# First score maximum ahead of the normalisation, and last score block ahead of the transposes with the maximum, in a fused cross-attention and mixture-of-experts kernel

## What is computed

```python
x = x + tanh(g_xattn) * xattn(layernorm(x), ctx, pos, pos, Wq, Wkv, Wout, bout)
x = x + tanh(g_ffn) * ffn(layernorm(x), sw1, sb1, sw2, sb2, rw1, rb1, rw2, rb2, router_w, router_b)
# xattn: q, k rotated; logits = q k^T / sqrt(8); w = softmax(logits); (w v) @ Wout + bout
# ffn: mean of 2 shared experts + sum over the 6 best of 32 routed experts of gate * expert(x)
```

## Time and profile before

| | |
|---|---|
| median of 3 runs | 428.22 us (428.2 to 428.32) |
| the profiled execution | 428.19 us, of which 426.2 us are the span from first to last instruction |
| busy: PE, DVE, ACT, POOL | 407.9, 264.4, 192.3, 154.5 us |
| granted PE clock over the span | 0.998 of full speed |
| DMA | 39.42 MB, mean 92 GB/s |

### The profile page before, as it was taken

The page is one execution under the profiler, slowest core; times in us unless marked ns, Lnnn a source line. Parts: engine busy times, 40 slices in busy tenths (PEclk is TensorE's granted clock), DMA queues, the critical chain, the costliest instruction groups (busy, mean ns, idle before and its releaser), DMA issues.

```text
span 426.2 us, 8239 instructions
## 1 busy us (share of the span) xinstructions
PE 407.9 (96%) x2651; PEld 315.9 (74%) x2651; DVE 264.4 (62%) x525; ACT 192.3 (45%) x371; POOL 154.5 (36%) x296
## 2 busy tenths in 40 slices
PE   7799999999999889999999999999999999999995
PEld 5477766666666567788888888888888888888884
DVE  7987888788887476365555555555555555555554
ACT  4784999889888736322222222222222222222221
POOL 8446333311001026344433443333433444444430
PEclk9999999999999999999999999999999999999999
DMA  8300000000000069399876333333333232333102
GB/s 227 87 2 0 2 3 2 2 2 2 2 2 2 2 179 339 95 240 262 242 221 210 98 98 98 96 99 90 94 93 105 77 105 86 95 97 96 49 0 99
DMA packets 27992, 39.42 MB, mean 92 GB/s; under 512 B 3665, under 2 KB 22145, under 8 KB 27969
## 3 DMA queue, kind: packets, MB, share of 16 engines
q1 hardware_dynamic: 26929, 39.11, 32.4%
q10 hardware_dynamic: 1040, 0.01, 0.1%
HBM read 37.93 MB, written 1.18 MB: 92 GB/s over the span
## 4 chain that ended last, share of the span: by engine, by line
PE 63%; DVE 1%; ACT 0%; DVEq 0%; issue 0%; ACTq 0%
PE psum L1255 30%; PE psum L1272 30%; PE psum L1231 1%; PE psum L968 0%; DVE attn L955 0%; PE psum L1225 0%; PE psum L1169 0%; PE psum L1292 0%; DVE xT L947 0%; DVEq L78 0%; PE psum L1157 0%; ACT Vx L583 0%; PE psum L1286 0%; PE psum L1125 0%; ACT lgT L646 0%
## 5 line engine op out<-in xcount | busy, mean ns | idle before, releaser
L669 ACT ACTIVATE hh<-hu 128x512 fp32r<-128x512 f32 x88 | 55.7, 633 | 182.1 <-DVE hu L936 182.1
L936 DVE SCALAR_TENSOR_TENSOR hu<-psum,b1cols,G 128x512 f32<-128x512 f32 x88 | 65.9, 750 | 105.2 <-PE psum L1255 101.7
L824 DVE TENSOR_REDUCE nmax<-psum 128x2 f32<-128x512 f32 x128 | 79.4, 683 | 11.1 <-PE psum L1067 10.4
L550 ACT ACTIVATE probs<-psum 128x512 f32<-128x512 f32 x128 | 69.4, 597 | 12.5 <-PE psum L1085 11.3
L1272 PE MATMUL psum<-hh,w2h 128*128 128x512 f32 x188 | 73.3, 390 | 0.0
L1272 PE MATMUL psum<-hh,w2l 128*128 128x512 f32 x188 | 73.2, 389 | 0.0
L1272 PE MATMUL psum<-hl,w2h 128*128 128x512 f32 x188 | 73.2, 389 | 0.0
L942 DVE SCALAR_TENSOR_TENSOR hl<-hu,hh 128x512 fp32r<-128x512 f32 x88 | 61.1, 696 | 9.2 <-ACT hh L669 9.2
L469 POOL CAST w2h<-w 128x256 fp32r x44 | 17.5, 398 | 126.7 <-PE psum L1272 126.7
L1255 PE MATMUL psum<-xTh,w1h 128*128 128x512 f32 (+1 forms) x188 | 58.1, 390 | 0.0
L1255 PE MATMUL psum<-xTh,w1l 128*128 128x512 f32 (+1 forms) x188 | 57.9, 389 | 0.0
(11 more groups left out here) (147 smaller groups left out, 487.0 us busy)
## 6 DMA issues: line engine op xcount, KB each, us to landing
w<-in_L_ffn_rw_dram SPq DMA_DIRECT2D x8, 1408.0 KB, 10.1
G<-gates_by_expert SPq DMA_DIRECT2D x40, 256.0 KB, 4.0
G<-gates_by_expert SPq DMA_DIRECT2D x8, 448.0 KB, 3.6
G<-gates_by_expert SPq DMA_DIRECT2D x8, 384.0 KB, 3.5
G<-gates_by_expert SPq DMA_DIRECT2D x8, 320.0 KB, 3.6
G<-gates_by_expert SPq DMA_DIRECT2D x8, 192.0 KB, 3.9
x_sb<-in_x_dram SPq DMA_DIRECT2D x4, 256.0 KB, 4.2
G<-gates_by_expert SPq DMA_DIRECT2D x8, 128.0 KB, 3.8
```

The costliest lines, as they stand in the source:

```text
L550: act.activation(probs[g % 2][:, :, n, :], st_bank(g, n)[:, :].rearrange("p (t q) -> p t q", t=TB), ACT.Exp, scale=SCALE).then_inc(exp_ok, 1)
L669: act.activation(hh[(SHT + j) % 2][:, cols], hu[2 * j + half][:, :], ACT.Relu).then_inc(rhh_ok, 1)
L824: dve.tensor_reduce(nmax[i % 2][:, :, n], S_BANK[(4 * i + n) % SB][:, :].rearrange("p (t k) -> p t k", t=TB), AX.X, ALU.max, negate=True). ...
L936: dve.scalar_tensor_tensor(out=hu[2 * (j % 2) + half][:, :], in0=H_BANK[2 * (j % 2) + half], scalar=b1cols[:, bass.ds(it * len(G) + j, 1)] ...
```

## The change

In DVE's loop the first maximum of a step comes ahead of `normalise` and of `residual`. In PE's loop, in odd steps from 7 on, `transposed_with_max` comes behind the last score block instead of ahead of it. Nothing is added or left out.

```diff
             for i in range(GROUPS + 4):
+                if i < GROUPS:
+                    row_max(i, 0)
                 if i >= 7 and i % 2:
                     normalise((i - 7) // 2)
                 if i - 1 in PROJ_STEPS:
                     residual(*PROJ_STEPS[i - 1])
                 if i < GROUPS:
-                    row_max(i, 0)
                     row_max(i, 1)
                     row_max(i, 2)
                     row_max(i, 3)
@@
                 if i >= 6 and i % 2 == 0:
                     outputs((i - 6) // 2)
-                if i >= 1:
+                outputs_read = i >= 7 and i % 2 == 1
+                if i >= 1 and not outputs_read:
                     transposed_with_max(i - 1)
                 if shifted:
                     pairs(score(i, 3), shifted_score(i - 2, 0))
                     pairs(shifted_score(i - 2, 1))
                 else:
                     pairs(score(i, 3))
+                if outputs_read:
+                    transposed_with_max(i - 1)
                 if weighted:
                     values(i - 3)
```

## The result

The changed kernel takes 436.81 us in the median (433.55 to 439.99, 4 executions), before it was 428.22: slower by the factor 1.0198, 95% interval 1.0154 to 1.0243. The forecast was 433.7 us with a range to 435.0. The direction was right, the time lies above the range. The four executions fall into two pairs: 433.55 and 433.91 us at a granted clock of 0.998 and 0.997, 439.70 and 439.99 us at 0.978. The first pair is the forecast. The profile is of an execution of the second pair (439.70 us), so it shows both what the forecast had and what it lacked. Executions more than 1.5% above their kernel's fastest are in the medians of this document, but not in its factors, which concerns one execution of `e9_residual_only_again` and two of `e7_longer_stall`.

What follows compares the result with a forecast made beforehand. The prediction took PE to bound the kernel, through the length of its attention steps. Odd steps +1.6 us and four residual stalls +3.9 us gave +5.5 us on 428.22, so 433.7 us, range 431.8 to 435.0.

Steps and rivals of the forecast that it cites:

- Part 1: Odd attention steps 7 to 31: moved transposes, taken as 0.30 us, put values at S + 2.43; together +1.6 us.
- S: Start of an attention step, that of its first score on PE; times within the step count from it in us.
- Part 2: Steps 16, 18, 24, 26: residual behind first maximum puts transposes at S + 1.83, values at S + 3.12; +3.9 us.
- The stall is not caught up: Opposite of a rival: PE catches up the residual's stall in four even steps, leaving 429.8 us; chance 0.05.
- The heavier rival: Stalled even steps hand their delay to the next odd step: 0.3 more in each of four, 434.9 us; chance 0.06.
- the rival on the clock: Attention: stalls lower PE's clock to 1.2 GHz, doubling 3.1 us of work four times; +12 us, 446 us; chance 0.02.
- the sum: Odd steps +1.6 us and the four residual stalls +3.9 us give +5.5 us, so 433.7 us; chance 0.70.

Runs made afterwards that it cites:

- e9_residual_only_again: Kernel before with only the residual behind the first maximum in steps 16, 18, 24, 26, run again; median 434.03 us, factor 1.0120.
- e7_longer_stall: The change with the residual one maximum later still, behind row_max(i, 1); median 443.37 us, factor 1.0301.
- e1_odd_only: The change in odd steps only, with the residual again ahead of the first maximum as in the kernel before; 430.28 us, factor 1.0048.
- e4_early_query_copy: Kernel before, with ACT's copy of the queries moved between two exponentials in even steps from 6 on; 426.12 us, factor 0.9958.
- e2_residual_only: Kernel before with only the first maximum ahead of the residual in steps 16, 18, 24, 26; 433.02 us, factor 1.0121.
- e5_change_again: The change run again without any edit, 6 executions; median 434.47 us, factor 1.0147 against the kernel before.
- e8_maximum_first_only: Kernel before with only DVE's half in odd steps, first maximum ahead of the normalisation, PE's order and residual as before; 434.45 us, factor 1.0168.
- e10_pe_order_only: Kernel before with only PE's half, transposes with the maximum behind the shifted scores in odd steps; 432.14 us, factor 1.0100.
- e6_stall_filled_short: The change with 4 dummy matmuls on PE ahead of the transposes that wait for the residual; 433.19 us, factor 1.0113.

## Why the prediction was right or wrong

- **Direction, and the time while the clock holds**: right. The executions of the change at 0.997 and more took 433.5 to 433.9 us, with one of 435.30, against 433.7. What made that one longer at a clock of 0.997 is open.
- **Part 1, + 1.6 us**: right in mechanism and size. Last score at S + 1.35 (1.34 forecast), values at S + 2.44 (2.43), transposes 0.30. In e1_odd_only it is 1.66 us. That the values could not use the earlier last score, because the exponential sets their start, and that the moved transposes then come on top, e4_early_query_copy bears out: it too brings the first maximum forward to S + 0.61 (61.32 - 60.71), leaves the transposes where they were, and gains 2.1.
- **Part 2, + 3.9 us**: right. Transposes at S + 1.83 as forecast, values at S + 3.07 (3.12), since they follow the transposes by 1.24 and not by 1.29. The sum is 3.8 us. The stall is not caught up.
- **The heavier rival** (a stalled step hands on its delay) exists, but only where the odd steps are those of before: 0.4 us in e2_residual_only, and none in the change, whose odd steps wait for the exponential anyway.
- **The step that failed is the rival on the clock**, to which I gave a chance of 0.02 and 446 us; the sum had the clock at nothing. It came in 2 of 4 executions and later in 2 of 6, and in the first trace it cost about 6 us. Those two executions of four take the median to 436.81. The argument read "shows 1.00 through all of the attention's waits". But those waits were short: between 31.5 and 142 us, the longest for which PE's records name a releaser was 0.4 us.

```profile
PE psum L1067 <- DVE nmax L824: 2.8, 15, 0.3
PE psum L1099 <- DVE attn L840: 0.5, 2, 0.4
```

I had worked out four idle stretches of about 1 us, and no wait in those steps was near that length. The Trainium skill (TensorE: Matmul & The Clock Gate, section "What's actually happening") says that missing activity brings the throttle back; I cited it and then set it aside by rows that hardly bore on it. The trace now agrees in the direction, with 0.50 after a stall.
- **What I overlooked: longer waits elsewhere in the same trace.** PE of the kernel before waits for 1.62 us in the projections and for 1.25 us at the end of the attention, and the granted clock is 1.00 around both:

```profile
20.87 0.92 PE L1008 MATMUL psum<-wq_sb,xnT 128*128 128x256 f32 x3 [1.62 <-ACT xnT L492]
...
151.33 0.41 PE L1125 MATMUL psum<-ident,oT 128*128 128x128 f32 x2 [1.25 <-DVE attn L840]
```

```profile
19.00:21.00 2.00, 0.38 (x4) 0.14 (x3) 2.00 (x4) 2.00 (x6) 2.00 (x2) 1.00 0.00 0
...
150.00:152.00 2.00, 0.76 (x10) 0.70 (x7) 1.28 (x11) 0.38 (x1) 1.33 (x1) 1.00 0.00 0
```

With these rows the chance of 0.02 would have looked better founded, and it would have been wrong all the same. The waits of 1.3 to 1.6 us at this place in the projections passed at 1.00 in every other trace too. So the length of one idle stretch does not decide by itself; what else there must be, no run shows.
- **The size of the clock's cost** was wrong too. I let the PE work of the four stalled steps double, + 12 us. In the trace the lower level covers steps that have no stall, 19 to 21 and the end of 18, and step 20 takes 5.09 us where it took 3.13 before (99.14 to 102.27), a factor of 1.6.

What decides in which executions the clock falls stays open. The same program at the same places shows both, so it is not the schedule alone. That the stalls behind the residual are enough to bring the falls about is shown: by e9_residual_only_again, which has the odd steps of before (3 of 6 executions, and none of 11 before), by e7_longer_stall (6 of 6), and by the traces, in which all falls in the attention but one, in e5_change_again, come at or right behind such a stall. That the odd steps play no part, and that work in the gap prevents the fall, is likely but rests on few executions.

## What to carry to other kernels

When work moves ahead on an engine, look for everything it was moved past: here the gain was sought at the normalisation, and the residual beside it in the same loop held up PE in four steps. Moving transposes out of a wait and behind another one makes them visible; ask first which wait ends last once the first is shortened. And before you write that the clock will hold, ask whether the trace has idle stretches as long as the new ones, in the same stage and amid the same work. Here it had none in the steady steps, while longer ones in other stages, 1.62 and 1.25 us with the clock at 1.00, would have misled. Where nothing comparable exists, the lower clock deserves more than a small chance, and several executions of the changed kernel tell more than one.

## What the runs showed of the hardware that was not expected

- With four stalls of 1.1 us in otherwise dense attention steps, PE's clock went from 2.4 to 1.2 GHz in 7 of 20 executions (the change and e2/e9 together). In two traces the level then lasted for about 17 us (98 to 115 us in the trace above), though PE was busy for 2.00 of 2.00 us there; in the trace of e5_change_again it lasted for 7 us, and again for 3. With stalls of 1.7 us the clock fell in 6 of 6, with PE kept busy in them in none of 9. One execution of e8_maximum_first_only, whose longest wait in these steps is 1.3 us, fell too (439.57 us, 0.981); with 0.9 us at most (e10_pe_order_only) none of 4 did. Yet single waits of 1.62 and 1.25 us outside these steps, which the kernel before has at 19 and 150 us, were at 1.00.
- At the lower level a step of 3.1 us takes 5.1 (step 20), so not twice as long. The values do take nearly twice as long (1.87 instead of 1.00 us to the next step's start), but from the last score to the values it is 0.73 instead of 0.63, a piece in which PE waits for the exponential at the full clock. Step 20 after the change, then before:

```profile
106.52 0.58 PE L1068 MATMUL psum<-QK 32*128 32x256 f32 x1
...
107.25 1.94 PE L1115 MATMUL psum<-probs,Vx 128*32 128x256 f32 x16
109.12 0.58 PE L1068 MATMUL psum<-QK 32*128 32x256 f32 x1
```

```profile
100.64 0.38 PE L1067 MATMUL psum<-QK 32*128 32x256 f32 x1
...
101.27 1.07 PE L1114 MATMUL psum<-probs,Vx 128*32 128x256 f32 x16
102.27 0.38 PE L1067 MATMUL psum<-QK 32*128 32x256 f32 x1
```

- Dummy matmuls in a wait cost nothing when the last of them starts in time, and the transposes behind them started even earlier after the residual (87.17 against its end at 87.11, in e6_stall_filled_short, where 0.15 was usual). Why wasn't tried.
